# Layer 0's input normalisation in a block of its own, and the state's additions after convolution groups 9 to 12

## The chip, the cores and the metric

The kernel runs on one core of a Trainium2 chip. The metric is device time in microseconds (us). Three runs of the kernel before took 7157.63, 7158.09 and 7130.31 us, median 7157.63 us.

## The reference, cut to what matters

Two layers are applied to x of 16 batches, 512 tokens and 256 channels, in f32. The first layer is a gated delta-rule recurrence with a small mixture of low-rank experts beside it; the second is an attention with a linear layer beside it. The change touches only how the first layer's normalised rows reach the recurrence and when the recurrence's state is added to.

```
xn = layernorm(x)                                     # per row of 256
q, k, v = silu(causal_conv4(xn @ W{q,k,v}.T) + b)      # 16 heads of 64, k scaled by 64**-0.5
a, beta = sigmoid(xn @ Wa.T + ba), sigmoid(xn @ Wb.T + bb)
for every token:                                      # S: 64 x 64 for each batch and head
    err = S k - v
    S   = a * S - beta * outer(err, k)
    o   = S q
x = x + gated_layernorm(o) @ Wo.T + experts(xn)
...                                                   # layer 1
```

## The kernel before, in words

The program has two parts, `layer0_recurrence` and `layer0_end_and_layer1`, each with its own `Block`, so that the second starts when the first has ended on all engines. Every engine writes its own stream of instructions and the streams meet in counted semaphores.

**The slots.** The recurrence cuts 512 tokens into 32 chunks of C = 16 and the batches into two groups of 8. One step is one chunk of one group, 64 steps in all, and the engines work through slots: in slot s the solve for step s runs beside the projections and convolutions for steps s+1 and s+2. The slots 4 to 59 are a hardware loop of two slots a turn (`slot_loop`). The two groups alternate, and each group's state lies in its own tile `st`.

**VectorE (DVE), `slot` at L947.** In this order: nine convolution groups of step s+1 (`conv`, L833, four multiply-adds of 128x128 each, groups 0 to 8); the first half of the solve (`half`, L890, eight tokens, starting with the copy at L911, which waits for the products `kp` of that step); `decay` (L848), which multiplies the whole state of the other group; then what stands between the halves; then the second half, which starts at L904 and waits for `xk`, what the first half's tokens contribute to the second half's. Between the halves `norm` (L865) normalises the input rows of step s+3: 13 small dependent instructions from the statistics (L876) to the normalised rows (L888). Each link of that chain calls `between_halves`, which puts one convolution group (9 to 17) between the links. After the groups in `STATE_AFTER_TAPS = (9, 12, 14, 16)` it also adds two of the eight parts of the state's update to `st` (`state`, L855, two instructions at L862), from the two banks `d_bank`.

**TensorE (PE), `slot` at L598.** In order: transpose of the rows of step s+2 (L538), a gate projection, `project` (L585) of the convolution banks 3, 4, 5 of step s+1 with `update` 0 and 1 between them, `cross` (L570), `update` 2, `project` bank 0 of step s+2, `update` 3, `project` bank 1, transposes of v (L514), `products` (L517), two more transposes, `project` bank 2, `scores`. `update(p)` (L486, matmuls at L502) makes two parts of the state's update in the two `d_bank` banks, and waits until the two parts before have been added (`d_freed`). `cross` waits for `xe`, the first half's result read back through HBM. `project` of bank 0 for step s+2 waits for the silu of convolution bank 3 of step s+1, that is, for groups 9, 10, 11; bank 1 waits for the silu of bank 4 (groups 12, 13, 14). `products` (L530) comes after the transposes that need the silu of bank 5 (groups 15, 16, 17).

**ScalarE (ACT), `slot` at L777.** The part that matters: silu of bank 3, `place_keys` (L682), `crossed` (L718: two copies out of `cross`'s banks, each followed by its write to `x_dram`), the writes of gates and betas, silu of bank 4, `evict` (L649) of banks 0 and 1 of step s+2, silu of bank 5, `values` with the write of `v_dram` (L699), the copies of `products` (L738) with the write of `prod_dram` (L744).

**SyncE (SP), `slot` at L301.** It issues the loads in a fixed order and stops at each wait. After the first half: e_dram write, `xe` load (tile `vt`, L346); then `xk` (L350), two broadcast loads of the decay (L359, 1 MB each), the input rows of step s+4 (`load_x`, L297, waits until `norm` of step s+3 has freed the single tile `xt`), `vb` (L368, waits for the write of `v_dram`), `upd_dram` (L375, waits for the end of the second half), `kp` (L386, waits for the write of `prod_dram`) and `qp`.

```
def between_halves():
    k = next(groups, None)
    if k is not None and front:
        conv(s + 1, k)
    if k in STATE_AFTER_TAPS and update:
        for u in range(2):
            state(s - 1, 1 - g, 2 * STATE_AFTER_TAPS.index(k) + u)
```

Of the kernel before, what the change touches and what calls it, by code (L numbers as in the profile page):

```python
# [10 lines left out]
B, T, HID = 16, 512, 256  # L11
H, DK, DV, TAPS = 16, 64, 64, 4
HD = H * DV
C = 16
GB = 8
GROUPS = B // GB
P = GB * C
# [7 lines left out]
EPS = 1e-5  # L25
# [5 lines left out]
def front1_use(s):  # L31

    return 4 * s if isinstance(s, int) and s < 2 else F_START + F_USES * (s - 2)
# [25 lines left out]
STATE_AFTER_TAPS = (9, 12, 14, 16)  # L59
# [30 lines left out]
RSQRT_STEPS = 3  # L90
NORM_OPS = 6 + 2 * RSQRT_STEPS

# [21 lines left out]
def due(value):  # L114

    return not isinstance(value, int) or value > 0
# [7 lines left out]
def held(engine, passed):  # L124

    engine.sem_inc(passed, 1)
# [31 lines left out]
def layer0_recurrence(nc, ins, o_dram):  # L158
# [12 lines left out]
    x = ins["L0_attn_x"]  # L171

    with ExitStack() as ctx:
        def sb(name, shape, dt=f32):
            return ctx.enter_context(nc.sbuf_tensor(name, shape, dt))
# [4 lines left out]
        def sem(name):  # L180
            return ctx.enter_context(nc.semaphore(name))
# [12 lines left out]
        xt = sb("xt", [P, HID])  # L194
        xn = sb("xn", [P, HID])
# [33 lines left out]
        norm_work = sb("norm_work", [P, 12])  # L229
        bst, mv, var, rs, rstmp, mhalf = (norm_work[:, a:b] for a, b in ((0, 6), (6, 8), (8, 9), (9, 10), (10, 11), (11, 12)))  # L230
# [20 lines left out]
        xn_ready, norm_chain = sem("xn_ready"), sem("norm_chain")  # L251
# [20 lines left out]
        def valid(lo, hi):  # L272
            return 0 <= lo and hi < STEPS
# [6 lines left out]
        def _(sp):  # L280
# [194 lines left out]
        def _(pe):  # L475
# [58 lines left out]
            def transposed(s, g):  # L534
                bank = use(front1_use(s), 0)
                pe.wait_ge(xn_ready, s + 1)
                for k in range(2):
                    mm = nc.tensor.transpose(bank[:, 128 * k:128 * k + 128], xn[:, 128 * k:128 * k + 128], ident[:])  # L538
                mm.then_inc(f_filled, 1)
                pe.wait_ge(f_freed, front1_use(s) + 1)  # L540
# [57 lines left out]
            def slot(s, n, g, lo, hi):  # L598
                front, ahead, state = valid(lo + 1, hi + 1), valid(lo + 2, hi + 2), updates(lo - 1, hi - 1)
                before = s - 1, n - 1 + g, 1 - g  # L600
                if ahead:
                    transposed(s + 2, g)
                    gate(s + 2, g, 0)
# [212 lines left out]
        def _(dve):  # L816
# [7 lines left out]
            nc.vector.tensor_reduce(batch_mask[:], own[:, :, 0], AX.XY, ALU.add).then_inc(norm_chain, 1)  # L824
            dve.wait_ge(norm_chain, 1)
# [38 lines left out]

            def norm(s, n, g, meanwhile):  # L865

                base, made = NORM_OPS * s + 1, [0]

                def link(ins):
                    made[0] += 1  # L870
                    ins.then_inc(norm_chain, 1)
                    meanwhile()
                    dve.wait_ge(norm_chain, base + made[0])

                dve.wait_ge(x_in[g], 16 * (n + 1))
                link(nc.vector.bn_stats(bst[:], xt[:]))  # L876
                held(dve, dve_passed)
                link(nc.vector.bn_aggr(mv[:], bst[:]))
                link(nc.vector.tensor_scalar(var[:], mv[:, 1:2], EPS, None, ALU.add))
                link(nc.vector.tensor_scalar(mhalf[:], mv[:, 1:2], EPS, -0.5, ALU.add, ALU.mult))  # L880
                link(nc.vector.tensor_scalar(rstmp[:].bitcast(i32), var[:].bitcast(i32), 1, None, ALU.logical_shift_right))
                link(nc.vector.tensor_scalar(rs[:].bitcast(i32), rstmp[:].bitcast(i32), -1.0, RSQRT_MAGIC, ALU.mult, ALU.add))
                for _ in range(RSQRT_STEPS):
                    link(nc.vector.tensor_scalar(rstmp[:], rs[:], rs[:], mhalf[:], ALU.mult, ALU.mult))
                    link(nc.vector.tensor_scalar(rs[:], rstmp[:], 1.5, rs[:], ALU.add, ALU.mult))
                if due(s):
                    dve.wait_ge(f_filled, front1_use(s - 1) + 1)
                nc.vector.tensor_scalar(xn[:], xt[:], mv[:, 0:1], rs[:], ALU.subtract, ALU.mult).then_inc(xn_ready, 1)  # L888
# [58 lines left out]
            def slot(s, n, g, lo, hi):  # L947
# [19 lines left out]
                if valid(lo + 3, hi + 3):  # L967
                    norm(s + 3, n + 1 + g, 1 - g, between_halves)
# [105 lines left out]
def layer0_end_and_layer1(nc, ins, o_dram, out):  # L1074
# [907 lines left out]
def program(nc, ins, out):  # L1982
    o_dram = nc.dram_tensor("o_dram", [T, B, H, DV], f32).ap()
    layer0_recurrence(nc, ins, o_dram)
    layer0_end_and_layer1(nc, ins, o_dram, out)
# [15 lines left out]
```

## Time and profile before

| what | value |
|---|---|
| runs of the kernel before | 7157.63, 7158.09, 7130.31 us; median 7157.63 |
| span of the profiled execution | 7152.7 us (its own time stands in no table; the span is 4.9 us under the median) |
| recurrence | to about 4292 us of the span |
| DVE, PE, POOL, ACT busy over the whole span | 76%, 70%, 51%, 46% |

The page of the profile describes one execution. A busy share is an average over stages, so what an engine's work is worth has to be read in the slot: which wait ends last there. In the timeline an entry has its start, its duration, the engine, the line, the operation with output and input, and in brackets the idle time before it with what ended it. Entries of one line are merged (x4, x32). The time of a matmul's end is modelled.

### The profile page before, as it was taken

The numbers are of one execution on the slowest core, as the hardware profiler recorded it, in microseconds if no ns is written. First come the engines' busy times: TensorE is split into PE (matmuls) and PEld (weight loads), VectorE is DVE, ScalarE is ACT, GpSimd is POOL, SyncE is SP. The second block draws the span as 40 slices with busy tenths as digits, with TensorE's granted clock in tenths as the row PEclk, the third lists the DMA queues.
The fourth block names the chain that finished last, engine by engine and source line by source line (L and its number), as shares of the span: only waits on it lengthen the run. The fifth ranks groups of instructions, "written<-read, shape, count | busy, mean of one in ns | idle before, by whom it ended". The sixth has DMA issues, their size and how long they took to land. (4 is left out here: it accounts for less than half of the span.)

```text
span 7152.7 us, 175742 instructions
## 1 busy us (share of the span) xinstructions
PE 5027.7 (70%) x58695; PEld 3318.4 (46%) x58695; DVE 5415.6 (76%) x15973; ACT 3322.6 (46%) x7234; POOL 3637.4 (51%) x4232
## 2 busy tenths in 40 slices
PE   5666666666666766666666644888878878888878
PEld 3555555555455555555555533333444443434443
DVE  5888889888888988888888864666666666666665
ACT  4554455444445444544454422444444444444444
POOL 3778778777777877787778771111111111111110
PEclk8777778777777777877777767888888888888888
DMA  4667666766766676667667742111111111111111
GB/s 124 156 158 163 165 152 160 167 160 148 166 162 161 158 166 163 155 158 170 153 157 164 170 107 64 43 50 51 45 45 44 44 48 44 44 44 44 44 45 37
DMA packets 1186126, 804.64 MB, mean 112 GB/s; under 512 B 1038563, under 2 KB 1090435, under 8 KB 1177220
## 3 DMA queue, kind: packets, MB, share of 16 engines
q1 hardware_dynamic: 878212, 610.17, 35.3%
q10 hardware_dynamic: 307200, 185.09, 10.6%
q8 instruction: 431, 7.06, 0.4%
q14 instruction: 283, 2.32, 0.1%
HBM read 490.57 MB, written 304.55 MB: 111 GB/s over the span
## 5 line engine op out<-in xcount | busy, mean ns | idle before, releaser
L464 POOL TENSOR_TENSOR qp<-qp,ab 128x512 f32<-128x512 f32 (+7 forms) x1024 | 937.3, 915 | 75.3
L469 POOL TENSOR_TENSOR qp<-qp,pt 128x512 f32<-128x512 f32 (+7 forms) x1024 | 912.8, 891 | 82.2 <-issue 2.0
L1771 DVE TENSOR_REDUCE nmax<-w_bank 128x1 f32<-128x512 f32 x1024 | 642.8, 684 | 408.0 <-PE w_bank L1353 403.1
L844 DVE SCALAR_TENSOR_TENSOR p_bank<-y,conv_w,p_bank 128x128 f32<-128x128 f32 x3072 | 828.1, 349 | 74.6 <-issue 25.0
L466 POOL TENSOR_TENSOR pt<-qp,vb 128x512 f32<-128x512 f32 (+7 forms) x1024 | 813.3, 794 | 9.2 <-DVE vb L921 9.2
L1308 POOL TENSOR_TENSOR ot<-ot,ln_w 128x1024 f32<-128x1024 f32 x64 | 151.1, 2361 | 1139.9 <-ACT ot L1610 1139.9
L530 PE MATMUL d_bank<-st 64*32 64x80 f32 x16384 | 490.1, 290 | 338.4 <-issue 319.1
L1313 POOL TENSOR_TENSOR x1b<-x,bias 128x256 f32<-128x256 f32 x64 | 46.4, 725 | 1162.7 <-DVE bst L1867 1162.7
L594 PEld LDWEIGHTS p_bank<-xnT,wqkv 128*128 128x128 f32 x4096 | 547.2, 215 | 192.2 <-issue 192.2
L502 PE MATMUL d_bank<-xd,kt 32*64 32x128 f32 x7936 | 342.4, 320 | 409.8 <-DVE st L862 393.2
L594 PE MATMUL p_bank<-xnT,wqkv 128*128 128x128 f32 x4096 | 596.5, 306 | 43.0 <-ACT st L676 31.3
L530 PEld LDWEIGHTS d_bank<-st 64*32 64x32 f32 x16384 | 437.9, 141 | 386.1 <-issue 383.4
L1584 ACT ACTIVATE pt<-e_bank 128x1024 f32<-128x1024 f32 x512 | 515.4, 1023 | 178.7 <-PE e_bank L1383 177.8
L1353 PE MATMUL w_bank<-ks,qs 96*128 96x512 bf16 x1024 | 398.6, 458 | 158.2 <-DMA ks<-part_dram 129.9
L738 ACT ACTIVATE prod<-d_bank 128x320 f32<-128x320 f32 x512 | 221.7, 438 | 592.8 <-PE d_bank L530 585.4
L502 PEld LDWEIGHTS d_bank<-xd,kt 32*64 32x64 f32 x7936 | 274.0, 160 | 453.6 <-issue 437.8
L655 ACT ACTIVATE y<-halo 128x96 f32<-128x96 f32 x384 | 114.2, 297 | 752.3 <-PE p_bank L594 652.6
L461 POOL TENSOR_TENSOR qp<-qp,xk 128x512 f32<-128x512 f32 x64 | 87.2, 1363 | 685.6 <-DMA xk<-x_dram 685.6
L844 DVE SCALAR_TENSOR_TENSOR c_bank<-y,conv_w,c_bank 128x128 f32<-128x128 f32 x1536 | 420.2, 352 | 13.6 <-ACT c_bank L663 13.6
L594 PE MATMUL c_bank<-xnT,wqkv 128*128 128x128 f32 x2048 | 319.2, 321 | 137.5 <-ACT z L679 132.7
L1610 ACT ACTIVATE ot<-ot,nmr,rs_b 128x64 f32<-128x64 f32 x1024 | 363.8, 437 | 96.2 <-DVE xn_b L1826 96.2
L663 ACT ACTIVATE p_bank<-p_bank,conv_b,conv_w 128x128 f32<-128x128 f32 x1024 | 378.9, 430 | 8.6
(219 smaller groups left out, 11769.4 us busy)
## 6 DMA issues: line engine op xcount, KB each, us to landing
db<-decay_dram SPq DMA_DIRECT2D x124, 1024.0 KB, 12.3
prod_dram<-prod ACTq DMA_DIRECT2D x64, 1280.0 KB, 9.7
kp<-prod_dram SPq DMA_DIRECT2D x64, 640.0 KB, 4.4
qp<-prod_dram SPq DMA_DIRECT2D x64, 640.0 KB, 6.5
a_dram<-at ACTq DMA_DIRECT2D x64, 512.0 KB
ab<-a_dram SPq DMA_DIRECT2D x64, 512.0 KB, 5.9
v_dram<-vt ACTq DMA_DIRECT2D x64, 512.0 KB
vb<-v_dram SPq DMA_DIRECT2D x64, 512.0 KB, 7.1
```

What stands on the lines that cost most here:

```text
L464: link(nc.gpsimd.tensor_tensor(q, q, ab[:, g, r:r + 1, :].to_broadcast([128, w, DV]), ALU.mult), 1)
L466: link(nc.gpsimd.tensor_tensor(pt2[:, 0:w], qp[:, g, r:r + w, DV + r:DV + r + 1].to_broadcast([128, w, DV]), vb[:, g, r:r + 1, :].to_broad ...
L469: link(nc.gpsimd.tensor_tensor(q, q, pt2[:, 0:w], ALU.add))
L502: last[e] = nc.tensor.matmul(d_bank[e][64 * par:64 * par + 64, 128 * k:128 * k + 128], kt[32 * q:32 * q + 32, g, DK * h:DK * h + DK], xd[3 ...
L530: mm = nc.tensor.matmul(d_bank[b % 2][at_:at_ + 32, ROW * hq:ROW * hq + ROW], slot_[:, DV:DV + 2 * C], slot_[:, 0:ROW], start=True, stop=True)
L594: mm = nc.tensor.matmul(bank[:, 128 * i:128 * i + 128], wqkv[:, k, 128 * m:128 * m + 128], xnT[:, g, k, :], start=k == 0, stop=k == 1)
L663: last = nc.scalar.activation(bank[:, 128 * i:128 * i + 128], bank[:, 128 * i:128 * i + 128], ACT.Identity, bias=conv_b[:, m:m + 1], scale ...
L844: nc.vector.scalar_tensor_tensor(out=zz, in0=y[:, j % Y_BANKS, i, :, tap:tap + C], scalar=conv_w[:, m, tap:tap + 1], in1=zz, op0=ALU.mult, ...
L1353: nc.tensor.matmul(bank[:], qs[0:ROWS, h, 128 * t:128 * t + 128], ks[0:ROWS, h, :], start=True, stop=True).then_inc(filled, 1)
L1584: nc.scalar.activation(pt[:, kt % 2, 2 * pr:2 * pr + 2], e_bank[pr][:], ACT.Exp, scale=float(D1) ** -0.5).then_inc(e_freed, 1)
L1610: last = nc.scalar.activation(o[:, h, :], o[:, h, :], ACT.Identity, bias=nmr[:, h:h + 1], scale=rs[:, h + 1:h + 2])
L1771: nc.vector.tensor_reduce(nmax[:, n:n + 1], bank[:], AX.X, ALU.max, negate=True).then_inc(freed, 1)
```

## The change: what it does, and its diff

A new function `normalise_rows` runs as a block of its own ahead of the recurrence. It loads all 8192 rows of x in eight pieces of 1 MB on SP's queue, computes on DVE eight row statistics and a chain of dependent small operations per piece (eight values wide), applies scale and bias on ACT (eight activations of 128x256 per piece), and writes the normalised rows to a new tensor in HBM, `xn_dram`. The recurrence loads its rows from there into a tile with one slice for each group; `norm` is gone from DVE, PE's transpose waits for the load instead, and SP's `load_x` waits for the transpose of step s+2 instead of for `norm`. `STATE_AFTER_TAPS` becomes (9, 10, 11, 12). The second part of the program takes `xn_dram` as an argument but goes on computing its own normalisation.

```
-STATE_AFTER_TAPS = (9, 12, 14, 16)
+STATE_AFTER_TAPS = (9, 10, 11, 12)
...
+def normalise_rows(nc, x, xn_dram):
+    pieces, per = 8, B * T // (8 * 128)
+    src, dst = (a.rearrange("b t c -> (b t) c").rearrange("(p n k) c -> n p k c", n=pieces, k=per) for a in (x, xn_dram))
...
+        @block.sync
+        def _(sp):
+            for n in range(pieces):
+                sp.dma_start(rows[:, n], src[n]).then_inc(rows_in[n], 16)
+            for n in range(pieces):
+                sp.wait_ge(rows_normed, n + 1)
+                sp.dma_start(dst[n], normed[:, n]).then_inc(rows_wr[n], 16)
+            for n in range(pieces):
+                sp.wait_ge(rows_wr[n], 16)
...
+            for n in range(pieces):
+                dve.wait_ge(rows_in[n], 16)
+                for k in range(per):
+                    last = nc.vector.bn_stats(stats[:, n, k], rows[:, n, k])
+                link(last)
+                s = stats[:, n]
+                link(nc.vector.tensor_tensor(m2, s[:, :, 1], s[:, :, 4], ALU.add))
+                link(nc.vector.tensor_tensor(dm, s[:, :, 1], s[:, :, 4], ALU.subtract))
+                link(nc.vector.tensor_tensor(dm, dm, dm, ALU.mult))
+                link(nc.vector.tensor_tensor(vs, s[:, :, 2], s[:, :, 5], ALU.add))
+                link(nc.vector.scalar_tensor_tensor(out=vs, in0=dm, scalar=HID / 4.0, in1=vs, op0=ALU.mult, op1=ALU.add))
+                link(nc.vector.tensor_scalar(var, vs, 1.0 / HID, EPS, ALU.mult, ALU.add))
+                rsqrt_ops(nc, rs, var, t, link)
+                link(nc.vector.tensor_copy(scale[:, n, 0], rs))
+                nc.vector.scalar_tensor_tensor(out=scale[:, n, 1], in0=m2, scalar=-0.5, in1=rs,
+                                               op0=ALU.mult, op1=ALU.mult).then_inc(row_scales, 1)
...
+            for n in range(pieces):
+                act.wait_ge(row_scales, n + 1)
+                for k in range(per):
+                    last = nc.scalar.activation(normed[:, n, k], rows[:, n, k], ACT.Identity,
+                                                bias=scale[:, n, 1, k:k + 1], scale=scale[:, n, 0, k:k + 1])
+                last.then_inc(rows_normed, 1)
...
-        xt = sb("xt", [P, HID])
-        xn = sb("xn", [P, HID])
+        xn = sb("xn", [P, GROUPS, HID])
...
-                src = x[GB * g:GB * g + GB].rearrange("b (n t) c -> n b t c", t=C)
-                sp.dma_start(xt[:], src[bass.ds(n, 1)]).then_inc(x_in[g], 16)
+                src = xn_dram[GB * g:GB * g + GB].rearrange("b (n t) c -> n b t c", t=C)
+                sp.dma_start(xn[:, g], src[bass.ds(n, 1)]).then_inc(x_in[g], 16)
...
-                    if due(s + 4):
-                        sp.wait_ge(xn_ready, s + 4)
-                    held(sp, sp_passed)
+                    if not isinstance(s, int) or s + 2 >= 0:
+                        sp.wait_ge(f_filled, front1_use(s + 2) + 1)
+                        held(sp, sp_passed)
                     load_x(n + 2, g)
...
-            def transposed(s, g):
+            def transposed(s, n, g):
                 bank = use(front1_use(s), 0)
-                pe.wait_ge(xn_ready, s + 1)
+                pe.wait_ge(*dma_of(x_in, n, g, 0))
+                held(pe, pe_passed)
...
-                if valid(lo + 3, hi + 3):
-                    norm(s + 3, n + 1 + g, 1 - g, between_halves)
                 for _ in range(TAP_GROUPS):
                     between_halves()
```

`rsqrt_ops` (L129) is 14 dependent operations: two that make the first guess and three rounds of four.

## Rows read from the trace of the kernel before

**Rows 1.** The page, span of the profiled execution.

```profile
span 7152.7 us, 175742 instructions
```

**Rows 2.** The decay's instructions by their line: count, duration, first and last start.

```profile
L852 DVE TENSOR_TENSOR st<-st,db x62: 4752/4919/5239, 185.0 to 4188.1; 128x4096 f32<-128x4096 f32 x62
```

**Rows 3.** Who waited for whom: us in total, times, longest us.

```profile
PE d_bank L502 <- DVE st L862: 393.2, 63, 12.2
...
PE d_bank L530 <- issue: 319.1, 63, 7.6
DVE kp L904 <- DMA xk<-x_dram: 316.8, 64, 22.6
```

**Rows 4.** Timeline of DVE, the slot read: first us, then duration, line, what.

```profile
2028.49 4.76 DVE L852 TENSOR_TENSOR st<-st,db 128x4096 f32<-128x4096 f32 x1 [0.21 <-DVE eb L945]
...
2034.54 1.28 DVE L862 TENSOR_TENSOR st<-d_bank,st 128x512 f32<-128x512 f32 x2
...
2036.89 1.12 DVE L844 SCALAR_TENSOR_TENSOR p_bank<-y,conv_w,p_bank 128x128 f32<-128x128 f32 x4
...
2049.28 0.41 DVE L888 TENSOR_SCALAR xn<-xt,norm_work 128x256 f32<-128x256 f32 x1
2054.41 0.22 DVE L904 TENSOR_TENSOR kp<-kp,xk 128x64 f32<-128x64 f32 x1 [4.72 <-DMA xk<-x_dram]
...
2079.86 0.62 DVE L911 COPY rows_bank<-kp 128x448 f32<-128x448 f32 x1
```

**Rows 5.** Timeline of PE in the same slot.

```profile
2035.96 1.99 PE L502 MATMUL d_bank<-xd,kt 32*64 32x128 f32 x32 [8.09 <-DVE st L862]
2037.87 3.35 PE L580 MATMUL f_bank<-vt,sc 32*32 32x64 f32 x128
2041.15 1.17 PE L502 MATMUL d_bank<-xd,kt 32*64 32x128 f32 x32
2042.24 2.05 PE L594 MATMUL p_bank<-xnT,wqkv 128*128 128x128 f32 x16
...
2060.71 2.70 PE L530 MATMUL d_bank<-st 64*32 64x80 f32 x88 [4.60 <-issue]
```

**Rows 6.** Timeline of ACT in the same slot.

```profile
2038.05 0.60 ACT L679 ACTIVATE z<-p_bank 128x512 f32<-128x512 f32 x1 [5.65 <-DVE p_bank L844]
...
2041.92 0.59 ACTq L730 DMA_DIRECT2D x_dram<-prod  x1
...
2044.12 0.60 ACT L679 ACTIVATE z<-p_bank 128x512 f32<-128x512 f32 x1 [2.23 <-DVE c_bank L844]
...
2049.85 0.61 ACT L679 ACTIVATE z<-c_bank 128x512 f32<-128x512 f32 x1
```

**Rows 7.** Timeline of SP's queue in the same slot.

```profile
2046.59 0.36 SPq L350 DMA_DIRECT2D xk<-x_dram  x1
...
2072.77 0.33 SPq L386 DMA_DIRECT2D kp<-prod_dram  x1
```

**Rows 8.** ACT in a slot whose silu of bank 5 was late.

```profile
1650.83 0.61 ACT L679 ACTIVATE z<-c_bank 128x512 f32<-128x512 f32 x1
```

**Rows 9.** DVE around that late slot: its decay, the next first half, the next decay.

```profile
1626.92 4.76 DVE L852 TENSOR_TENSOR st<-st,db 128x4096 f32<-128x4096 f32 x1 [0.22 <-DVE eb L945]
...
1682.17 0.63 DVE L911 COPY rows_bank<-kp 128x448 f32<-128x448 f32 x1 [1.20 <-DMA kp<-prod_dram]
1695.23 4.93 DVE L852 TENSOR_TENSOR st<-st,db 128x4096 f32<-128x4096 f32 x1 [0.22 <-DVE eb L945]
```

**Rows 10.** PE's products in a slot without a pause in them.

```profile
2310.35 7.00 PE L530 MATMUL d_bank<-st 64*32 64x80 f32 x256
```

**Rows 11.** Groups of instructions by line: busy us, mean ns of one | idle before, releaser.

```profile
L876 DVE BATCH_NORM_STATS2 norm_work<-xt 128x6 f32<-128x256 f32 x64 | 26.6, 415 | 16.1 <-DMA xt<-in_L_attn_x 16.0
...
L137 DVE TENSOR_TENSOR rs_b<-rs_b,rstmp_b 128x17 f32<-128x17 f32 x192 | 34.3, 179 | 6.6
```

**Rows 12.** Stretch while weights load alone; last three: PE clock, DMA share, GB/s.

```profile
5.00:10.00 5.00, 0.00 (x0) 0.00 (x0) 3.82 (x3) 0.00 (x0) 0.00 (x0) 1.00 1.01 430
```

More of the change, by code:

```diff
@@ L155, in slot_loop, with sb, sem, _ @@
         slot(s, (s - s % 2) // 2, s % 2, s, s)
-def layer0_recurrence(nc, ins, o_dram):
+def normalise_rows(nc, x, xn_dram):
+    pieces, per = 8, B * T // (8 * 128)
+    src, dst = (a.rearrange("b t c -> (b t) c").rearrange("(p n k) c -> n p k c", n=pieces, k=per) for a in (x, xn_dram))
+    with ExitStack() as ctx:
+        def sb(name, shape):
+            return ctx.enter_context(nc.sbuf_tensor(name, shape, f32))
+        def sem(name):
+            return ctx.enter_context(nc.semaphore(name))
+        rows = sb("rows", [128, pieces, per, HID])
+        normed = sb("normed", [128, pieces, per, HID])
+        stats = sb("row_stats", [128, pieces, per, 6])
+        work = sb("row_work", [128, 6, per])
+        scale = sb("row_scale", [128, pieces, 2, per])
+        m2, dm, vs, var, rs, t = (work[:, i] for i in range(6))
+        rows_in, rows_wr = ([sem(f"{name}{n}") for n in range(pieces)] for name in ("rows_in", "rows_wr"))
+        row_chain, row_scales, rows_normed = sem("row_chain"), sem("row_scales"), sem("rows_normed")
+        block = ctx.enter_context(nc.Block())
+        @block.sync
[7 more added lines that the diff above has]
+                sp.wait_ge(rows_wr[n], 16)
+        @block.vector
+        def _(dve):
+            made = [0]
+            def link(ins_):
+                made[0] += 1
+                ins_.then_inc(row_chain, 1)
+                dve.wait_ge(row_chain, made[0])
+            for n in range(pieces):
[14 more added lines that the diff above has]
+                                               op0=ALU.mult, op1=ALU.mult).then_inc(row_scales, 1)
+        @block.scalar
+        def _(act):
+            for n in range(pieces):
[4 more added lines that the diff above has]
+                last.then_inc(rows_normed, 1)
@@ L159, in dram, with layer0_recurrence @@
+def layer0_recurrence(nc, ins, xn_dram, o_dram):
     def dram(name, shape):
@@ L532, in products @@
                     mm.then_inc(p_filled, 1)
-            def transposed(s, g):
+            def transposed(s, n, g):
                 bank = use(front1_use(s), 0)
-                pe.wait_ge(xn_ready, s + 1)
+                pe.wait_ge(*dma_of(x_in, n, g, 0))
+                held(pe, pe_passed)
                 for k in range(2):
-                    mm = nc.tensor.transpose(bank[:, 128 * k:128 * k + 128], xn[:, 128 * k:128 * k + 128], ident[:])
+                    mm = nc.tensor.transpose(bank[:, 128 * k:128 * k + 128], xn[:, g, 128 * k:128 * k + 128], ident[:])
                 mm.then_inc(f_filled, 1)
@@ L863, in state @@
                                         ALU.add).then_inc(d_freed, 1)
[L865 to L888, printed above, removed]
             def half(s, n, g, later):
@@ L1071, in turns, with layer0_end_and_layer1 @@
     body(B - 1, Turn(B - 1, True, False), True, False, False)
-def layer0_end_and_layer1(nc, ins, o_dram, out):
+def layer0_end_and_layer1(nc, ins, xn_dram, o_dram, out):
     x = ins["L0_attn_x"]
@@ L1983, in program @@
     o_dram = nc.dram_tensor("o_dram", [T, B, H, DV], f32).ap()
-    layer0_recurrence(nc, ins, o_dram)
-    layer0_end_and_layer1(nc, ins, o_dram, out)
+    xn_dram = nc.dram_tensor("xn_dram", [B, T, HID], f32).ap()
+    normalise_rows(nc, ins["L0_attn_x"], xn_dram)
+    layer0_recurrence(nc, ins, xn_dram, o_dram)
+    layer0_end_and_layer1(nc, ins, xn_dram, o_dram, out)
 def kernel(**inputs):
```

13 lines of the change are left out of this document (4 added, 9 removed).

## The prediction, made before the changed kernel was run

> **What bounds the kernel now.** I began with the page for the span [rows 1], then took the decay's line as a clock: 62 decays between 185.0 and 4188.1 us, one in each slot [rows 2], so 61 intervals of 65.6 us. Next the waits. DVE waits 316.8 us in all for `xk` before the second half, about 5 us a slot, and PE sits 393.2 us ahead of L502 until DVE has added the first parts of the state [rows 3]. So DVE has slack between the halves, and what it does there matters only through what it releases.
>
> The timelines of one slot show what that is. I count from T0 = 35.8, when the first pair of state additions ends (2034.54 + 1.28) [rows 4]; the decay began 7.3 before T0. DVE's own work between the halves ends at +13.9, `xk` lets the second half begin at +18.6, and nine convolution groups later the next first half starts at +44.0 [rows 4]. From there to the next decay are 12.3 us, so a slot is 44.0 + 12.3 + 7.3 = 63.6; the mean slot of 65.6 has its first half at about +46.
>
> Two paths run from T0 to the next first half.
> - The **xk path**: update 1 on PE from +0.1 to +2.1, cross from +2.1 to +5.4, update 2 until +6.5 [rows 5]. Convolution group 11 ends at +2.2 [rows 4], the silu of bank 3 starts at +2.2, and 3.9 us after it ACT issues the second write of `x_dram` at +6.1 [rows 6]. SP issues `xk` at +10.8 [rows 7] and DVE starts at +18.6.
> - The **kp path**: the silu of bank 5 at +14.0 [rows 6] releases v's transposes and the products, in which PE pauses 4.60 us without a releaser [rows 5] (319.1 us in 63 slots, 5.1 each [rows 3]); then `prod_dram` is written and `kp` issued at +36.9 [rows 7]. It arrives about when DVE wants it.
>
> A slot with a late silu of bank 5 shows what the second path does when it slips: the silu starts at 1650.83 [rows 8], 31.3 us later the first half starts, after a wait for `kp`, and that slot lasts 68.3 us [rows 9].
>
> **The change part by part.** *The new block.* Nothing overlaps it, since the parts are separate blocks. DVE does 64 statistics of 0.41 us, about 0.36 apart, and in each of eight pieces 22 small operations. The nearest row is L137, 17 wide instead of 8: 0.179 us each and 6.6 us idle over 192, 0.213 apart [rows 11]. A piece is 8 x 0.36 + 22 x 0.213 = 7.6 us, eight are 61. Ahead of that the first 1 MB must land (2.4 us at 430 GB/s [rows 12], with issue and landing about 4.5), behind it stand ACT's last eight activations (at the 0.41 of a 128x256 instruction [rows 4], about 3), the last store and its landing (about 4.5) and the passage to the next block (1): 74 us. The 16.8 MB of traffic takes 39 us at 430 GB/s and is hidden. Bounds: 60, if statistics and chain overlap; 100, if loads and stores together got only some 40% of the rate of rows 12. I take 74, as DMA has nothing else to do here, as in rows 12. The first slot no longer waits for its own chain of 13 instructions, which by the same rows is worth some 4 us. Net **+70**.
>
> *norm leaves DVE.* About 3 us of instructions a slot go, but they lie beside the wait for `xk`, so the wait grows by as much. What counts is that the statistics stood ahead of the first additions: T0 comes 0.3 earlier, -0.3 a slot. Once the cover is gone this would be worth 3 us.
>
> *The loads of rows.* Same size, same place in SP's queue. The old wait for norm is replaced by one for PE's transpose, which is long done; queued behind it are `vb`, `upd_dram`, `kp` and `qp`, none earlier or later for it, since `vb` waits for the write of `v_dram`. PE's transpose waits for a load two slots old. Zero.
>
> *The additions move up.* Each pair needs an update on PE, and these have not moved. From the new T0: group 10 ends at 1.0, but update 1 ends at 2.1, so DVE stands 1.1 us and adds until 3.4. Group 11 ends at 4.5 (before: 2.2). Pair 2 needs update 2, behind cross, which ends at 6.5: DVE stands 2.0, adds until 7.7, group 12 ends at 8.8. Update 3 comes after the projection of bank 0 (2.05 us [rows 5]), so not before 9.6: DVE stands 0.8, adds until 10.9, hardly sooner than before. Groups 13 and 14 end at 13.0, group 17 at 16.3, still ahead of `xk`. DVE's waits are covered; the silus queued behind the groups are not.
> - xk path: the silu of bank 3 goes from +2.2 to +4.5, and the second write of `x_dram` from +6.1 to +8.4. `xk` at 18.6 + 2.3 = +20.9, and without a wait for `kp` the next first half at 20.9 + 25.4 = +46.3.
> - kp path: the silu of bank 4 starts at +13.0 instead of +8.3, and the silu of bank 5 5.7 us behind it as now (2044.12 to 2049.85 [rows 6]), since two evictions lie between: +18.8 instead of +14.0. From it to the first half are 30.0 us in the slot read and 31.3 in the late one [rows 4, 6, 8, 9]. I take 30.2, nearer the first, because the write of `v_dram` no longer starts while `xk` is loading. First half at +49.0.
>
> The later one decides: 49.0 + 12.3 + 7.0 (the decay to the new T0) = 68.3 us, as long as the late slot lasts now. Against 65.6 that is +2.7, over 61 intervals **+165 us**. Both the pause and its place are uncertain: at 31.3 the slot is 69.4 (+232); with the pause gone the xk path holds and the slot is 65.6 (0).
>
> **Sum.** 7152.7 + 70 + 165 = 7388 as a span; the median of the runs is 4.9 above the span, so about **7393 us**, 3.3% slower.
>
> A rule speaks against this sum. The row shows PE standing 4.60 us inside the products with no releaser [rows 5]. The Trainium skill, "Runtime: NRT & Kernel Launch", section "Instruction fetch mechanics", says that the sequencer streams its instructions block by block and that crossing a block is mostly hidden. By that rule the pause would go and the kp path with it, which is rival A; rows 3 disagree, with 63 such pauses.
>
> **The rivals.** *A, the kp path is absorbed (0.20).* In one slot the 256 products run through in 7.00 us without a pause [rows 10]. If starting them 4.5 us later puts them behind the two decay loads, the pause falls away, and prod_dram is written no later than now. Then only the xk path remains, 46.3 + 12.3 + 7.0 = 65.6, and only the block is paid: 7157.6 + 70 = 7228 us, with some waits left up to 7290. Against it: the late slot.
>
> *B, everything passes on (0.15).* 31.3 us after a silu at +18.8, or with PE's pause at its worst of 7.6 [rows 3] instead of 4.6: +3.8 to +5.5 a slot, 7460 to 7565.
>
> *C, faster (0.05).* Mechanism: the write of `v_dram` (512 KB) leaves the stretch in which `xk` loads. `xk` now takes 7.8 us from issue to use [rows 4, 7]; at about half, 4.0, it would stand at +17.1, the first half at +42.5 if the products also lose their pause, and the slot would last 61.8: -3.8 x 61 + 70 = -162, 6996 us. It decides from 1.15 us a slot, the block's 70 over 61. For it: 512 KB at 430 GB/s [rows 12] are 1.2 us. Against it: the two decay loads of 1 MB still come right behind `xk`, and v_dram's write started only at the end of that stretch. The Trainium skill, "Trainium Kernel Development and Optimization", section "Key Constraints", says that the DMAs of SP's and ACT's queues share the same 16 engines and interleave, which is why a moved write can matter at all; no row here separates the two queues' shares.
>
> *D, about even (0.05).* As C with half of it: slots 0.6 to 1.7 us shorter pay for the block. *The change doesn't do what it says:* the additions are placed after groups 9 to 12, but by the working above the last ends at +10.9 where it now ends at +11.4; that is within the forecast, not beside it.
>
> **How the numbers follow.** The forecast (7330 to 7450) has 0.55, A 0.20, B 0.15, C and D 0.05 each. A measurement of this kernel tells about 0.5% (36 us) from no change. Slower: 0.55 + 0.20 + 0.15 = 0.90; same: 0.05; faster: 0.05. The range from 7220 to 7500 takes in A and the lower half of B and leaves out C, D and the rest of B.
>
> **What would show it.** Right: a block of 70 to 80 us ahead of everything, DVE-bound; decays 68 us apart; DVE waits of 1 to 2 us for L502 ahead of the second and third pair; the silu of bank 5 near +19; waits for `kp` in nearly every slot. Wrong: decays under 66 us apart (A or C), no pause in the products (A), `xk` sooner after its issue than 7 us (C), a block near 100 us (held by its DMAs), or a kp wait above 5 us (B).

## The result, and the profile after

The changed kernel takes 7402.4 us (median of four runs, 7393.8 to 7408.0) against 7144.1 for the kernel before (four runs, 7130.3 to 7158.1). The ratio is 1.0356, with a 95% interval from 1.0336 to 1.0376: slower by 3.6%, where 3.3% and 7393 us were forecast. The span of the profiled execution went from 7152.7 [rows 1] to 7392.0 us, +239.3; between the medians lie 258.3, as the profiled execution of the kernel before was one of its longer ones.

Two rows cut this sum into three: the page's span, and the decay's line with its first and last start.

```profile
span 7392.0 us, 174417 instructions
```

```profile
L914 DVE TENSOR_TENSOR st<-st,db x62: 4424/4762/5116, 249.8 to 4448.6; 128x4096 f32<-128x4096 f32 x62
```

Against 185.0 and 4188.1 [rows 2], the first decay comes 64.8 us later (the block and the filling of the pipeline), the 61 intervals grow from 65.6 to 68.8 us and cost 195.7, and what lies behind the last decay is 21.2 us shorter. The last number was in no forecast. It comes from one execution of each kernel and is taken up under e6.

The front, in the timelines of SP, DVE and ACT. The block's first load is issued at 0.75 us, as the recurrence's was before, and the recurrence's own first load now at 70.66: 69.9 us.

```profile
0.75 4.12 SPq L180 DMA_DIRECT2D rows<-in_L_attn_x  x8
16.64 50.03 SPq L183 DMA_DIRECT2D xn_dram<-normed  x8
70.66 0.41 SPq L351 DMA_DIRECT2D wqkv<-in_wqkv  x1
```

```profile
5.35 2.71 DVE L199 BATCH_NORM_STATS2 row_stats<-rows 128x6 f32<-128x256 f32 x8 [5.35 <-DMA rows<-in_L_attn_x]
...
12.46 2.71 DVE L199 BATCH_NORM_STATS2 row_stats<-rows 128x6 f32<-128x256 f32 x8
```

```profile
62.28 4.04 ACT L218 ACTIVATE normed<-rows,row_scale 128x256 f32<-128x256 f32 x8 [3.06 <-DVE row_scale L210]
```

DVE's eight pieces stand 7.1 us apart (12.46 - 5.35), and ACT waits for DVE in each. The block is bound by DVE, as forecast.

The waits of the changed kernel (us in all, times, longest), which answer to [rows 3]:

```profile
PE d_bank L563 <- DVE st L924: 401.0, 62, 11.6
DVE st L924 <- PE d_bank L563: 315.9, 186, 5.0
PE p_bank L656 <- ACT z L741: 261.3, 63, 5.3
DVE kp L941 <- DMA xk<-x_dram: 233.7, 63, 22.5
DVE rows_bank L948 <- DMA kp<-prod_dram: 192.3, 59, 6.1
PE d_bank L591 <- issue: 183.3, 61, 5.7
```

In the kernel before the second of these was 28.3 us and the fifth 67.3. The additions now wait for PE (5.1 us a slot), the first half waits for `kp` in 59 slots instead of 25, and the wait for `xk` has shrunk from 316.8 to 233.7. PE's pause in the products has shrunk from 319.1 to 183.3 us; in its place PE waits for the silu ahead of its projections.

One slot shows it in order. Its decay starts 3963.6, and T0, the end of the first pair, is 3970.7. DVE, which answers to [rows 4]:

```profile
3969.45 1.27 DVE L924 TENSOR_TENSOR st<-d_bank,st 128x512 f32<-128x512 f32 x2
...
3972.89 1.29 DVE L924 TENSOR_TENSOR st<-d_bank,st 128x512 f32<-128x512 f32 x2 [1.13 <-PE d_bank L563]
...
3977.66 1.29 DVE L924 TENSOR_TENSOR st<-d_bank,st 128x512 f32<-128x512 f32 x2 [2.44 <-PE d_bank L563]
...
3980.66 1.29 DVE L924 TENSOR_TENSOR st<-d_bank,st 128x512 f32<-128x512 f32 x2 [0.68 <-PE d_bank L563]
...
3991.17 0.23 DVE L941 TENSOR_TENSOR kp<-kp,xk 128x64 f32<-128x64 f32 x1 [4.05 <-DMA xk<-x_dram]
...
4019.76 0.63 DVE L948 COPY rows_bank<-kp 128x448 f32<-128x448 f32 x1 [3.00 <-DMA kp<-prod_dram]
```

The three bracketed waits (1.13, 2.44, 0.68) are those that were worked out as 1.1, 2.0 and 0.8; their means over all slots are 1.1, 3.0 and 1.0. DVE is still ahead of `xk` by 4.05 us. It is the wait of 3.00 for `kp` that lengthens the slot. ACT, which answers to [rows 6], and PE, to [rows 5]:

```profile
3975.25 0.60 ACT L741 ACTIVATE z<-p_bank 128x512 f32<-128x512 f32 x1 [6.87 <-DVE p_bank L906]
...
3984.06 0.60 ACT L741 ACTIVATE z<-p_bank 128x512 f32<-128x512 f32 x1 [5.30 <-DVE p_bank L906]
...
3991.09 0.61 ACT L741 ACTIVATE z<-c_bank 128x512 f32<-128x512 f32 x1
...
4005.38 0.39 ACTq L806 DMA_DIRECT2D prod_dram<-prod  x1
```

```profile
3977.53 2.05 PE L656 MATMUL p_bank<-xnT,wqkv 128*128 128x128 f32 x16
3979.51 1.10 PE L563 MATMUL d_bank<-xd,kt 32*64 32x128 f32 x32
3984.80 3.75 PE L656 MATMUL p_bank<-xnT,wqkv 128*128 128x128 f32 x16 [4.19 <-ACT z L741]
...
4001.60 3.27 PE L591 MATMUL d_bank<-st 64*32 64x80 f32 x89 [3.33 <-issue]
```

The silu of bank 3 starts at +4.5 (forecast +4.5), that of bank 4 at +13.3 (+13.0), that of bank 5 at +20.4 (+18.8). The last is late by something that no step foresaw: PE had stood 4.19 us, and the same 16 matmuls of the projection take 3.75 us instead of 2.05. The stretches of the two projections, with the granted clock in the third column from the end:

```profile
3977.50:3979.60 2.10, 2.10 (x24) 1.95 (x24) 1.94 (x5) 0.60 (x1) 1.60 (x5) 1.00 0.24 27
...
3984.80:3988.40 3.60, 3.60 (x17) 3.60 (x18) 2.33 (x9) 2.28 (x7) 0.00 (x0) 0.50 0.73 180
```

The granted clock is 1.00 in the first and 0.50 in the second, 2.4 and 1.2 GHz. Over all slots the second projection takes 2.05 us on the mean in the kernel before and 3.75 in the changed one, where it is slow in every one of 61.

### The profile page after: what moved, and what is told of

Read it like the earlier page. It is cut to its first block and busy times, and to the rows that moved or that the text cites. A ratio compares the mean times of both kernels' runs of the same rounds, so it can differ in the third digit from the quotient of the medians.

```text
span 7392.0 us, 174417 instructions
## 1 busy us (share of the span) xinstructions
PE 5079.6 (69%) x58695; PEld 3388.7 (46%) x58695; DVE 5347.7 (72%) x15381; ACT 3339.0 (45%) x7298; POOL 3638.5 (49%) x4232
## 3 DMA queue, kind: packets, MB, share of 16 engines
q8 instruction: 431, 7.06, 0.4%
## 5 line engine op out<-in xcount | busy, mean ns | idle before, releaser
L525 POOL TENSOR_TENSOR qp<-qp,ab 128x512 f32<-128x512 f32 (+7 forms) x1024 | 989.9, 967 | 79.8 <-issue 4.6
L530 POOL TENSOR_TENSOR qp<-qp,pt 128x512 f32<-128x512 f32 (+7 forms) x1024 | 932.8, 911 | 80.3
L656 PE MATMUL p_bank<-xnT,wqkv 128*128 128x128 f32 x4096 | 686.8, 337 | 295.9 <-ACT z L741 261.3
L656 PEld LDWEIGHTS p_bank<-xnT,wqkv 128*128 128x128 f32 x4096 | 633.7, 244 | 435.9 <-issue 435.9
L527 POOL TENSOR_TENSOR pt<-qp,vb 128x512 f32<-128x512 f32 (+7 forms) x1024 | 741.6, 724 | 9.3 <-DVE vb L958 9.3
L563 PE MATMUL d_bank<-xd,kt 32*64 32x128 f32 x7936 | 346.2, 323 | 438.6 <-DVE st L924 401.0
L591 PE MATMUL d_bank<-st 64*32 64x80 f32 x16384 | 492.6, 293 | 201.1 <-issue 183.3
L924 DVE TENSOR_TENSOR st<-d_bank,st 128x512 f32<-128x512 f32 x496 | 318.9, 684 | 315.9 <-PE d_bank L563 315.9
L563 PEld LDWEIGHTS d_bank<-xd,kt 32*64 32x64 f32 x7936 | 277.1, 161 | 482.2 <-issue 468.2
L741 ACT ACTIVATE z<-p_bank 128x512 f32<-128x512 f32 x128 | 76.4, 597 | 774.7 <-DVE p_bank L906 772.7
```

Source lines behind the costliest of these rows:

```text
L525: link(nc.gpsimd.tensor_tensor(q, q, ab[:, g, r:r + 1, :].to_broadcast([128, w, DV]), ALU.mult), 1)
L527: link(nc.gpsimd.tensor_tensor(pt2[:, 0:w], qp[:, g, r:r + w, DV + r:DV + r + 1].to_broadcast([128, w, DV]), vb[:, g, r:r + 1, :].to_broad ...
L530: link(nc.gpsimd.tensor_tensor(q, q, pt2[:, 0:w], ALU.add))
L563: last[e] = nc.tensor.matmul(d_bank[e][64 * par:64 * par + 64, 128 * k:128 * k + 128], kt[32 * q:32 * q + 32, g, DK * h:DK * h + DK], xd[3 ...
L591: mm = nc.tensor.matmul(d_bank[b % 2][at_:at_ + 32, ROW * hq:ROW * hq + ROW], slot_[:, DV:DV + 2 * C], slot_[:, 0:ROW], start=True, stop=True)
L656: mm = nc.tensor.matmul(bank[:, 128 * i:128 * i + 128], wqkv[:, k, 128 * m:128 * m + 128], xnT[:, g, k, :], start=k == 0, stop=k == 1)
```

## The experiments

Twelve kernels were run, each timed in turn with the kernel before on its chip. The table holds means over 61 slots, taken from the timelines of each; places are us after T0, and "pause" is PE's idle time inside the products with no releaser.

| kernel | ratio (95%) | slot | silu bank 5 | xk used | pause | prod_dram written | kp issued | first half | wait for kp |
|---|---|---|---|---|---|---|---|---|---|
| before | 1 | 65.6 | 14.6 | 18.9 | 5.2 | 29.7 | 39.8 | 45.4 | 1.0 |
| changed | 1.0356 (1.0336 to 1.0376) | 68.8 | 21.2 | 20.5 | 2.9 | 34.1 | 44.6 | 48.7 | 3.1 |
| e1 additions alone | 1.0310 (1.0281 to 1.0340) | 69.3 | 20.8 | 20.3 | 3.4 | 34.1 | 44.6 | 48.9 | 2.8 |
| e2 additions back | 1.0083 (1.0056 to 1.0110) | 65.9 | 15.7 | 19.5 | 5.2 | 30.8 | 40.7 | 45.9 | 1.4 |
| e4 pairs 2, 3 early | 1.0049 (1.0026 to 1.0073) | 66.4 | 15.1 | 18.9 | 5.6 | 30.7 | 41.3 | 46.0 | 1.4 |
| e5 banks 4, 5 late | 1.0198 (1.0167 to 1.0229) | 68.1 | 18.8 | 19.2 | 4.0 | 32.5 | 43.3 | 47.7 | 2.0 |
| e6 block alone | 1.0089 (1.0057 to 1.0121) | 65.5 | 14.8 | 19.0 | 5.4 | 30.0 | 39.9 | 45.3 | 1.1 |
| e7 update 3 first | 1.0367 (1.0333 to 1.0400) | 69.1 | 19.5 | 20.4 | 5.1 | 34.5 | 44.8 | 49.0 | 3.5 |
| e8 decay after vb | 1.0307 (1.0267 to 1.0347) | 68.9 | 14.4 | 18.0 | 0.8 | 24.0 | 43.5 | 48.4 | 3.6 |
| e9 decay after xk | 1.0247 (1.0214 to 1.0281) | 68.4 | 14.4 | 18.0 | 2.2 | 25.7 | 43.9 | 48.0 | 4.3 |
| e10 decay last | 1.0056 (1.0035 to 1.0076) | 66.3 | 17.7 | 20.7 | 0.7 | 27.2 | 37.4 | 45.9 | 0.1 |
| e11 as e10, changed | 1.0613 (1.0584 to 1.0642) | 72.0 | 27.2 | 24.4 | 0.4 | 36.9 | 47.9 | 52.1 | 2.6 |
| e12 decay before xk | 1.0126 (1.0104 to 1.0147) | 67.1 | 21.2 | 21.7 | 0.6 | 30.7 | 40.7 | 46.8 | 0.1 |
| e13 as e12, changed | 1.0635 (1.0612 to 1.0658) | 72.1 | 27.6 | 23.8 | 0.6 | 37.2 | 47.9 | 52.1 | 4.1 |

### Which part costs what: e1, e2, e6

The additions alone:

```
# the kernel before
-STATE_AFTER_TAPS = (9, 12, 14, 16)
+STATE_AFTER_TAPS = (9, 10, 11, 12)
```

> The kernel before, with the additions alone moved to after groups 9 to 12; norm stays on DVE, no block. Theory K (the kp path sets the slot: a late silu of bank 5, then products, prod_dram, kp): the slot grows as in the changed kernel, from 65.6 to about 69.0 us, because norm lies under DVE's waits; 7144 + 61 x 3.4 = about 7350 us, no gap at the front. Theory D (DVE's own waits add up, 5.1 us a slot, less the work of norm taken away): with norm kept as well the slot is 65.6 + 5.1 = 70.7 us or more, 7455 us. Theory X (only the xk path, +1.6 us a slot): 7240 us.

Measured: 1.0310, slots of 69.3 us, theory K. The slots grow by 3.7 us, more than the 3.2 of the whole change. With `norm` kept on DVE they are only 0.5 longer than without it, so most of the chain's 3 us does lie under other waits; D's 70.7 us did not come.

The block and the removal of norm without the moved additions (the changed kernel with the old tuple):

> The changed kernel with the additions back after groups 9, 12, 14, 16: the block and the removal of norm alone. Theory K: the block costs 65 us at the front, the slots gain at most the 0.3 us of the statistics ahead of the first additions (61 x 0.3 = 18): 7144 + 65 - 18 = about 7190 us, slots 65.3 us. Theory D: norm's 3 us a slot come off, 7144 + 65 - 180 = about 7030 us, faster than before.

Measured: 1.0083. D falls: it wanted a kernel faster than before. But K's own gain of 0.3 us a slot is missing too, for the slots are 65.9 instead of 65.6 us. T0 comes 7.1 instead of 7.5 us after the decay, yet PE's cross starts 9.6 us after the decay in both. The waits say why: in the kernel before 51.1 us in 6 waits, in this one

```profile
PE f_bank L642 <- DMA vt<-e_dram: 77.8, 38, 34.3
```

Cross is then held by the read of `xe` instead of by update 1. The 0.3 us bought a new wait, that of cross. DVE, sooner without `norm`, now waits for PE ahead of its later additions (106.7 us in all instead of 28.3), and the silu of bank 5 starts 22.8 us after the decay instead of 22.1.

The block by itself:

```
# the kernel before
+    xn_dram = nc.dram_tensor("xn_dram", [B, T, HID], f32).ap()
+    normalise_rows(nc, ins["L0_attn_x"], xn_dram)
     layer0_recurrence(nc, ins, o_dram)
```

> The kernel before with the new block put ahead of it and its result not used: the recurrence loads and normalises x as before. Theory: the block costs what it takes by itself, 70 us from the first instruction to the recurrence's first load (66 to 70), and everything behind it is unchanged: ratio about 1.0095, slots 65.6 us. Rival: the 17 to 22 us by which the second part of the program was shorter in both kernels with the block (2834 and 2840 us against 2857) come with the block or with the tensor behind it; then the ratio is about 1.007 and the second part shows it here too. If it is 2857 here, it came with the removal of norm.

Measured: 1.0089, slots 65.5 us, first decay at 255.0, 70.0 us later than before. The parts nearly add up: 0.0310 for the additions and 0.0089 for the block make 0.0399, and the whole is 0.0356, which would leave some 0.4%, about 30 us, as given back by the removal of norm. The three intervals are 0.2 to 0.3% wide to each side, so this difference is no larger than they leave open.

In the traces a part of it is not in the recurrence. The second part of the program starts with the load of `wg`. In the timeline of SP this load stands in the kernel before, in the changed kernel and in e6 at

```profile
4296.03 0.38 SPq L1233 DMA_DIRECT2D wg<-in_wg  x1
```

```profile
4557.64 0.40 SPq L1268 DMA_DIRECT2D wg<-in_wg  x1
```

```profile
4358.35 0.39 SPq L1300 DMA_DIRECT2D wg<-in_wg  x1
```

From there to the end of the spans (7152.7, 7392.0, 7221.8) are 2856.7, 2834.4 and 2863.5 us; in e1 2857.8, in e2 2839.9. The second part is 17 to 22 us shorter in these two kernels without norm and not in the one with the block alone. But each figure is one execution, and over all fourteen traces the two kinds overlap: 2846.0 to 2863.5 us in the nine kernels with norm, 2834.0 to 2851.9 in the five without (2851.9 in e11). What goes with the time is TensorE's granted clock: over the second part it is 0.86 in the changed kernel, 0.85 in the kernel before and 0.84 in e6, and PE's busy time there, for the same 9671 matmuls, is 2228, 2253 and 2269 us. So it isn't shown that norm's absence has a part in it. Nor is the gain of norm's removal seen in the whole: e2 is as fast as e6 (1.0083 and 1.0089) because slots 0.4 us longer (65.9 against 65.5, 23 us over 61) met a second part 24 us shorter.

### Are DVE's waits the cost, or what stands behind them: e4, e5

```
# e4, the kernel before
-STATE_AFTER_TAPS = (9, 12, 14, 16)
+STATE_AFTER_TAPS = (9, 12, 13, 14)
# e5, the kernel before
                     if k is not None and front:
                         conv(s + 1, k)
+                    if k == 11 and front:
+                        nc.vector.tensor_reduce(spare[:], wqkv[:, 0], AX.X, ALU.add)
```

> The kernel before with the additions after groups 9, 12, 13, 14: DVE has to wait for updates 2 and 3 of PE (about 2 us a slot by the working), but groups 11 and 14 are hardly later than now (silu of bank 3 at +2.3, of bank 4 at about +9, of bank 5 near +15). Theory K: no change, 7130 to 7190 us, slots 65.6 to 66.2 us, although DVE's waits ahead of L862 rise from 0.4 to about 2 us a slot. Theory D: each us of wait is paid, +1.6 us a slot, 7240 us.

> The kernel before with one added DVE instruction after group 11 in each slot, a reduction over 3072 constants into a spare column (about 3.2 us); nothing reads its result. Groups 12 to 17 and the last three pairs come 3.2 us later, group 11 and with it the xk path stay. Theory K: silu of bank 5 at about +17.5 instead of +14.6, products and kp follow, the first half from +45.4 to +47.5: slots of about 67.7 us, 7144 + 61 x 2.1 = about 7270 us, with xk no later after T0 than now (18.9). Theory X: the xk path alone sets the slot and DVE still ends ahead of xk: 7144 to 7165 us.

In e4 DVE stands 2.2 us a slot ahead of its additions instead of 0.4 and the silus move by 0.5 to 1.0 us. The ratio of 1.0049 is 35 us (by the decays of the profiled execution 0.8 us a slot, 46 us), and the clearest part of it is the `kp` path (issue at 41.3 instead of 39.8). D's 1.6 us a slot are not there, K's "no change" is not quite either: half a microsecond at bank 5 passed on.

In e5 the added instruction takes 3.34 us and releases nothing:

```profile
L965 DVE TENSOR_REDUCE spare<-wqkv 128x1 f32<-128x3072 f32 x64 | 213.7, 3340 | 0.0
```

`xk` is used at +19.2, practically where it was, and DVE still waits for it. The silu of bank 5 goes to +18.8, `kp` is issued 3.5 us later, and the slot grows by 2.5 us. A late `kp` path, with the xk path where it was, makes a slot of 68 us: that is shown. The xk path alone is not what sets it.

### PE's pause takes back what is gained ahead of it: e7

```
# the changed kernel, PE
-                if ahead:
-                    project(s + 2, g, 0)
                 if state:
                     update(*before, (3,))
+                if ahead:
+                    project(s + 2, g, 0)
```

> The changed kernel with PE's update 3 ahead of the projection of bank 0. Theory K with the clock: PE no longer stands 4.2 us before the projection of bank 1, so that this one runs at full clock (2.05 us instead of 3.75); pair 3 is added 0.7 us sooner; the silu of bank 5 goes from +21.2 to about +19, and the pause in the products (2.9 us) takes back about half of it: slots 67.6 instead of 68.8 us, 61 x 1.2 = 70 us less, about 7330 us on the changed kernel's 7402. If the pause takes back all of it: 7380 to 7400. If the order of the two does not matter to the silu: unchanged.

Measured: 1.0367, no different from the changed kernel (1.0356). The silu of bank 5 does come 1.7 us sooner, and the products start 1.8 sooner; the waits of e7 then have

```profile
PE d_bank L591 <- issue: 317.5, 65, 6.9
```

against 183.3. The pause is 2.2 us longer and `prod_dram` is written at 34.5 instead of 34.1. The forecast of "about half" was wrong: all of it went. So the end of the pause hardly hangs on when the products begin: PE goes on 30.4 us after T0 on the median, against 30.9 in the changed kernel. The other half of the expectation failed too: the slow clock did not go but moved, from the projection of bank 1 to that of bank 0 (3.52 and 2.02 us in the slot read, 3.57 and 2.07 on the mean).

### What the pause waits for: e8, e9, e10, e12

Four places for the decay's two 1 MB loads on SP's queue; the computation is the same. e8 behind `vb`, e9 where they were but after a wait for `xk`, e10 at the end of the slot, e12 right behind the read of `xe`. The moved lines, and e9's added wait:

```
                 if updates(lo, hi):
+                    sp.wait_ge(*dma_of(xk_in, n, g, 0))      # e9 only
+                    held(sp, sp_passed)                      # e9 only
                     sp.wait_ge(*dma_of(dec_wr, n, g, 0))
...
                     for par in range(2):
                         rows = decay_dram[g][par:par + 1].to_broadcast([64, GB * HP, DV])
                         sp.dma_start(db[64 * par:64 * par + 64], rows).then_inc(db_in[g], 16)
```

> The kernel before with the two 1 MB loads of the decay moved on SP's queue from right behind xk to behind vb; nothing is left out. Theory P (PE's pause in the products, xk's 7.5 us and v_dram's 14 us of landing are waits for DMA engines busy with the decay loads): the pause of 5.2 us a slot shrinks below 2, xk is used under 6 us after its issue, vb is issued well before +31, and the slots shrink by 2 to 4 us, 120 to 240 us less, unless the moved loads now delay prod_dram and kp. Rival (the pause is a cost of PE's instruction stream by itself): the pause stays near 5 us wherever the loads are, the first half is held by kp as now, and the time is within 40 us of 7150.

> The kernel before with SP waiting for xk to land before it issues the two decay loads. Theory P: xk is used about 4 us after its issue instead of 7.5, so the xk path shortens by 3 us; the pause stays (the loads now start at about +16 and still lie over the products), so the kp path becomes the one that ends last in every slot: slots 64.5 to 65.5 us, 10 to 70 us less. Rival: as much again is lost in a longer pause, 7150 to 7250 us.

> The kernel before with the two decay loads moved to the end of SP's slot, behind kp and qp; nothing is left out. Behind vb the loads took PE's pause away (5.2 to 0.8 us) but held up prod_dram and kp (19.5 us from one issue to the other instead of 10.1). Theory P (both come from DMA engines busy with the decay loads): now neither happens, prod_dram is written at about +24, kp is issued when the second half has ended (about +35), and only the xk path is left: xk at +18, first half at +44, slots 63.5 to 64.5 us, 60 to 120 us less, ratio 0.983 to 0.992. Rival: the loads then hold up xd, ab, or e_dram and the read of xe, and the decay or T0 comes late: slots 66 us or more.

> The kernel before with the two decay loads ahead of xk on SP's queue, right behind the read of xe: issued at about -2 (when the decay has freed the tile) instead of +12. Nothing is left out. In the trace of the kernel before the DMA engines are idle from about +1 to +5 (share 0.00 and 0.04). Theory P (PE's pause, and xk's and prod_dram's long landing, come from DMA engines busy with these loads, so the best place is where the engines are idle): pause below 2 us, prod_dram written at about +25, kp issued behind the second half (+35), xk at +18 or before, slots 63.3 to 64.5 us: 7157 - 61 x 1.7 = about 7050 us, ratio 0.980 to 0.990. Rival: the loads now hold up the read of xe or the writes of x_dram (which the xk path needs) by as much as they free later: 7120 to 7250 us.

The gain did not come in any of the four, and the mechanism held in part. What theory P said of the pause in the products held in e8, e10 and e12. What it said of `xk` did not: used 6.8 us after its issue in e8 and 6.7 in e9, against 7.5 before and the forecast 4 to 6, so the decay loads right behind `xk` make up little of its landing time. With the loads behind `vb` the pause falls from 5.2 to 0.8 us and `prod_dram` is written 5.7 us sooner, but its landing, by the page's DMA issues 9.7 us in the kernel before, is

```profile
prod_dram<-prod ACTq DMA_DIRECT2D x64, 1280.0 KB, 20.3
```

and `kp` is issued 3.7 us later than before (1.0307). In e9 the landing of `prod_dram` takes 18.6 us, and the pause has not gone but moved behind the products, into the matmuls of the scores (L565), where the kernel before had 35.9 us in 11 waits:

```profile
PE f_bank L565 <- issue: 291.3, 60, 7.2
```

In e10 no first half waits for `kp` any more; now the rows of the update and `xe` are late, where the kernel before had 16.6 and 51.1 us:

```profile
PE d_bank L502 <- DMA xd<-upd_dram: 431.0, 57, 11.5
PE f_bank L580 <- DMA vt<-e_dram: 247.9, 64, 36.0
```

In e12 the loads fill the stretch where the DMA engines were idle, and most of PE's pause moves with them, from the products into the updates. Of the 44 pauses over 1.5 us there, 28 are in update 2 (113.5 us) and 16 in update 3 (38.6 us). DVE's additions then wait for PE 5.9 us a slot instead of 0.5, and the silu of bank 5 comes at +21.2 though no addition was moved:

```profile
PE d_bank L502 <- issue: 163.1, 53, 5.1
PE d_bank L530 <- issue: 37.4, 23, 3.9
```

So each place of the loads has something behind them on the path. The pause in the products shrinks in all four. It comes back at other matmuls in e9 and e12, but not in e8 and e10 (51.0 and 26.6 us in the scores).

What PE waits for in the pause can be read from the DMA packets of the trace. Those of the kind "instruction" on the queue that goes with PE's pauses (q8 on the page: 431 packets, 7.06 MB) are of 16 KB each, some six or seven a slot. In the slot read, PE stops in the products at 2056.11; such a packet runs from 2057.70 to 2059.03, and PE goes on at 2060.71. In the kernel before there are 60 pauses of over 1.5 us in the products. In every one of them such a packet ends, and PE goes on 1.5 us behind its end (median; 1.3 to 1.7 in nine of ten). In 55 of the 60, PE stops at the same two places of the code, after 168 of the 256 products in one slot of the loop's turn and after 198 in the other. The changed kernel's 51 pauses there, nearly all of e9's 60 in the scores and e12's 44 in the updates look the same. So the pause is PE waiting for its next instructions. In the kernel before, in e9 and in e12 the packet starts while the second decay load is in flight, 4.0, 5.4 and 2.9 us before its landing (medians). That these loads are what makes the packet late is argued from this and from the moves above.

The same packets show a second pause that no forecast had: at the first transposes of the loop's turns,

```profile
PE f_bank L538 <- issue: 147.7, 27, 6.9
```

27 times in 28 turns, with PE going on 1.8 us behind a packet. It stays wherever the decay loads are (147.3 to 181.5 us in all kernels), and no run tried what would remove it.

The Trainium skill, "Runtime: NRT & Kernel Launch", section "Instruction fetch mechanics", says that the sequencer fetches its stream by a DMA queue of its own while it executes, and the packets agree. Its "mostly hidden" holds for most of the packets here, and not for the one in the products, at 5.2 us a slot. The Trainium skill, "Trainium Kernel Development and Optimization", section "Key Constraints", says that SP's and ACT's DMAs share 16 engines; e8 agrees, with ACT's write of `prod_dram` at 20.3 us instead of 9.7.

### The changed kernel with the loads elsewhere: e11, e13

The same two moves (e10's and e12's) on the changed kernel.

> The changed kernel with the decay loads at the end of SP's slot. Theory K (the additions cost what they do because they push the kp path, which then ends last): with that path 10 us shorter the late silu of bank 5 (+21) is hidden (prod_dram at about +30, kp by +40, needed at +46), and only the xk path's +1.6 is left of the move: slots 65 to 65.7 us against 64 of the same loads in the kernel before, so 1.5 us a slot (90 us) and the block instead of 3.2 us a slot. Rival: the additions cost 3 us a slot wherever the loads are (slots 67 us or more).

> The changed kernel with the decay loads ahead of xk. Theory K: the moved additions cost what they do by pushing the kp path; with the pause gone that path has about 6 us to give, so of 3.2 us a slot only the xk path's 1.6 is left: slots of about 65.5 us, 200 us under the changed kernel, about 7200 us with the block. Rival: the additions keep their 3 us a slot against the same loads in the kernel before (slots 67 us, 7300 us), because the late silu of bank 5 is not hidden even then.

Theory K fell in both, and the rival's price of 3 us was too low as well: 72.0 and 72.1 us a slot, against 66.3 and 67.1 for the same loads with the old places. The changed kernel costs 5.7 and 5.0 us a slot there, not 1.6. The waits of e11 show what was left out of the forecast:

```profile
DVE st L924 <- PE d_bank L563: 689.8, 186, 9.5
PE f_bank L642 <- DMA vt<-e_dram: 363.7, 64, 32.2
```

PE's update 2 stands behind cross, and cross waits for `xe`. With the loads in the way `xe` lands late, and DVE, which now wants pair 2 after group 11, stands still with six convolution groups behind it (11 us a slot of waits for L563). In the old order three more groups ran first. In e13 DVE's waits are as long (707.1 us), with less of a wait for `xe` (203.7) and PE's own pauses in the updates beside it (145.7). The price of the early additions is not a fixed 3 us: it is the lateness of whatever PE waits for, handed to DVE.

## Why the prediction was right, and where not

**Bounds and paths.** Right: DVE had slack between the halves, two paths ran from T0 to the next first half, and the `kp` path came to end last (waits for `kp` in 59 slots). e5 shows it with the xk path left in place.

**The block, +74 and 4 back, net +70.** Measured 69.9 to the recurrence's first load and 64.8 to the first decay. DVE's pieces took 7.1 us instead of 7.6 (eight statistics in 2.71 us, and links 0.20 apart), ACT's last eight 4.04 instead of 3. The size was right to 5 us.

**norm leaves DVE, nothing.** The total came so (e2 and e6 are the same within their intervals), by luck in part: the slots grew by 0.4 us and the second part was shorter by as much. The step "-0.3 a slot" failed: cross waits for `xe` by then. With the additions moved as well, norm's removal is worth 0.5 us a slot (e1 against the changed kernel).

**The additions, +2.7 a slot, 165 us.** Measured +3.2, 196 us, and in e1, where they are moved alone, +3.7. The silu of bank 3 (+4.5) and `xk` (+20.9; 20.5) were right. Three terms were off.
- The silu of bank 5 came at +21.2 instead of +18.8. Half of that is pair 2, for which DVE stands 3.0 us on the mean instead of the 2.0 worked out, so that the silu of bank 4 comes at +14.2 instead of +13.0. The other half is "5.7 us behind it as now", which was 7.0: the projection of bank 1 ran at the slow clock after PE's idle time.
- "I take 30.2" from it to the first half was 27.5 (before, 30.8 on the mean). The pause shrank from 5.2 to 2.9 us, and the time from the issue of `kp` to the first half from 5.7 to 4.1, as `kp` had been waiting for DVE in many slots. So the first half came at +48.7 instead of +49.0.
- "12.3" from the first half to the next decay was 13.1 on the mean (12.7 before). That is where the missing half microsecond of the slot lies; what lengthened it wasn't looked into.

The first two cancelled. e7 shows why the pause did its part in that: sooner products only made a longer pause. That their sizes matched so nearly was luck.

**Rivals.** A (pause absorbed) and C (faster by moving v_dram's write) did not come: the pause stayed at 2.9 us and `xk` took as long from issue to use as before (20.5 - 12.8 = 7.7; before 18.9 - 11.4 = 7.5). B did not come because the pause shrank.

**The part behind the recurrence** was taken as unchanged; it gave some 22 us back in the one execution profiled, at a higher granted clock (0.86 against 0.85), and what raised it stays open.

**The sum.** That 7393 stands so near 7402 is partly luck: the block was put 5 us too high and the slots 30 us too low, and 21 us came off behind the last decay. The 4.9 us between span and median were not a cost either: in every run with both numbers on record the time is 1.8 us above the span, and the rest was the spread between executions.

## What to carry to other kernels

Before an operation is moved ahead, look at who feeds it: an engine that runs in order hands each wait to all that is queued behind the waiting instruction, so the price is read where that queue's results are next needed, here a chain of silu, products and two transfers, and not in the wait itself. Where a pause or a transfer absorbs lateness, it can absorb earliness too: the fix ahead of it (e7) was worth nothing. And where the DMA engines carry most of a loop's time, moving one large load only chooses what it delays; in four places it was never free.

## What the runs showed of the hardware that was not expected

- After 4.19 us of idleness TensorE ran the next 16 matmuls at a granted clock of 0.50 (3.75 us instead of 2.05). These 16 are as slow in all 61 slots, after 4.2 us of idleness on the mean. In the kernel before, the clock was 1.00 in the same projection of the slot read.
- TensorE stands still for 5.2 us a slot at a fixed place in its code, and goes on 1.5 us behind the landing of a 16 KB packet of its instructions. With two 1 MB loads moved elsewhere this pause shrank to 0.7 to 2.2 us in the products, and in two of four cases returned at other matmuls.
- The same wait stands at the return of the loop, 5.5 us each of 27 times, wherever those loads were.
- Putting those loads where the DMA engines had been idle cost 1.3%.
- The unchanged second part of the program took from 2834 to 2864 us over fourteen traces, shorter where its granted clock was higher (0.86 at 2834, 0.84 at 2864).
